# GpSimd scales weight pieces by multiplying two tensors, one of them a repeated column

## The chip, the cores and the metric

One core of one Trainium2 chip. The metric is the device time of one execution in microseconds, median of the runs. The kernel before took 574.97 us, median of 3 runs (567.21, 574.97 and 582.94). Engines are named as the profile names them: PE is TensorE's matmul side and PEld its weight loads, DVE is VectorE, ACT ScalarE, POOL GpSimd, SP the queue that issues most DMAs.

## The reference

One Flamingo-style layer: gated cross-attention, then a gated feed-forward layer with 8 experts of which each token uses 2. `x` is 8 x 256 x 256 (batch, tokens, width), the context 8 x 120 x 256.

```python
x = x + tanh(g_xattn[0]) * xattn(layernorm(x), ctx, w_q, w_kv, w_out, b_out)
x = x + tanh(g_ffn[0]) * ffn(layernorm(x), W1, W2, Wr)
# xattn: 16 heads of 64, softmax(q k^T / 8) v, then @ w_out + b_out
# ffn: the 2 best of 8 experts by softmax(x @ Wr^T), their weights renormalised,
#      y_e = silu(x @ W1[e]^T) @ W2[e]^T, out = sum of weight_e * y_e
# W1: (8, 1024, 256), W2: (8, 256, 1024)
```

Everything is float32 outside. The kernel keeps float32 accuracy with float16 matmuls: every operand is split into a high half and a low half (the rest that float16 could not hold), and a product is made of three matmuls.

## The kernel before

Attention runs over the 8 batches as one software pipeline: on each engine a list of steps is written out by hand inside a loop over p, and each step acts on batch p plus an offset. So order on an engine is fixed in the code, and engines meet through counting semaphores only. In the same loop the weights of the 8 experts are prepared, one expert per batch: SP loads `w1[q]` into `stage[0]` and `w2[q]` into `stage[1]` (each 128 x 2048 float32), ACT and PE find a bound from which DVE makes a power of two in `upw` (one column for W1, one for W2, the value repeated in all 128 partitions), ACT writes the high halves, and the low halves are made in chunks of 512 columns. In the trace this loop of weights covers roughly 46 to 285 us. After attention, 39 tiles of 128 gathered token rows go through the experts; tiles are added into `out` by an indirect DMA that accumulates, one after another.

Of an expert's eight chunks, four are made by DVE in one instruction each (line 1333: multiply by `upw`, subtract the high half) and four by POOL in two instructions each, in `split_low` of the GpSimd program (lines 630 to 641): line 637 scales the chunk in `stage` in place, then line 639 (W1) or 641 (W2) subtracts the high half and writes the float16 low half. A chunk is float32, 128 x 512. Between the two POOL waits on its own semaphore (`chain.link`), so that the second reads what the first wrote. With 8 experts there are 32 instructions on line 637, all in the loop.

POOL's other work in that loop, in program order around `split_low`: `p_low` (line 592, pT, the low half of the exponentials, a two-tensor subtraction of 120 x 512, eight per batch), `residual` (line 601), `scatter` (line 611, small indirect DMAs), and `norm2_factors` (lines 621 to 629, eight tiny instructions). What waits for them: PE's `values` (the matmuls o_bank<-v,pT) for `p_low`; SP's `store_w1` (line 436) for the low halves of W1, and `load_w` (lines 429 and 430), which fetches the next expert's W2 into `stage[1]`, for those of W2. ACT's `weight_sum` (line 885) then waits for that load.

```python
split_low(p + 7, 0, 1)
...
split_low(p + 7, 0, 3)
norm_factors(p + 8, 0)
p_low(p + 7, 0, 0)
...
p_low(p + 7, 0, 1)
...
split_low(p + 7, 1, 2)
...
split_low(p + 7, 1, 3)
p_low(p + 7, 1, 0)
```

Of the kernel before, what the change touches and what calls it, by code (L numbers as in the profile page):

```python
# [7 lines left out]
ALU = mybir.AluOpType  # L8
# [8 lines left out]
P = 128  # L17
# [150 lines left out]
def build(nc, x, ctxT, wq, wkv, wo, bo, gx, gf, w1, w2, wr, out, xn2_dram, table, w1_dram):  # L168
    ctx = ExitStack()
    with ctx:  # L170
# [3 lines left out]
        def sb(name, shape, dt, scope=ctx):  # L174
            return scope.enter_context(nc.sbuf_tensor(name, shape, dt))
# [26 lines left out]
        upw = [sb(f"upw{i}", [P, 2], F32) for i in range(2)]  # L202
# [179 lines left out]
        def w2_part(e, part, c, n=512):  # L382
            return w2s[:, e, part].rearrange("p c d -> p (c d)")[:, c:c + n]
# [138 lines left out]
        def _(pool):  # L522
            chain = Chain(pool, pool_chain)
# [107 lines left out]
            def split_low(q, i, k):  # L631
                if not 0 <= q < E:
                    return
                pool.wait_ge((w1_high, w2_high)[i][k // 2], q + 1)
                c = 512 * k
                chunk = stage[i][:, c:c + 512]
                chain.link(pool.tensor_scalar(chunk, chunk, upw[q % 2][:, i:i + 1], None, ALU.mult))  # L637
                if i == 0:
                    pool.tensor_tensor(w1_lo[:, k], chunk, w1_hi[:, c:c + 512], ALU.subtract).then_inc(w1_low[k], 1)
                else:  # L640
                    pool.tensor_tensor(w2_part(q, 1, c), chunk, w2_part(q, 0, c), ALU.subtract).then_inc(w2_low[k], 1)
# [58 lines left out]
            for p in range(-8, B + 3):  # L700
# [4 lines left out]
                tile_add(p + 4, 2)  # L705
                p_low(p + 6, 3, 1)
                split_low(p + 7, 0, 1)
                tile_gather(p + 6, 2)
                tile_gather(p, 12)
# [3 lines that stand above are left out]
# [8 lines left out]
                tile_add(p + 5, 0)  # L721
                constants(p + 8)
                split_low(p + 7, 1, 2)
                tile_add(p, 7)
                split_low(p + 7, 1, 3)
# [1364 lines left out]
```

## Time and profile before

| | |
|---|---|
| median of 3 runs | 574.97 us |
| lowest and highest run | 567.21 and 582.94 us |
| span of the profiled execution | 560.1 us |
| PE busy | 493.7 us (88%) |
| DVE busy | 370.2 us (66%) |
| ACT busy | 371.3 us (66%) |
| POOL busy | 363.9 us (65%) |

The span runs from the first to the last instruction; the page gives no total beside it, and the runs lie 7.1 to 22.8 us above it. Busy time is the union of an engine's instructions. A row of a timeline is: start in us, duration in us, engine, line, operation, output <- inputs with shapes, xcount, and in brackets the idle time before it and what ended it. A row of a group has, after the shapes, total busy us, mean ns of one, and the idle time before them. A row of the waits has total us, times, and the longest. The granted clock (PEclk) is a share of 2.4 GHz.

### The profile page before, as it was taken

How to read it: one execution, taken by the hardware profiler on the slowest of the kernel's cores; microseconds unless marked ns; L12 is line 12 of the kernel's file. 1: busy time of each engine (PE TensorE's matmuls, PEld its weight loads, DVE VectorE, ACT ScalarE, POOL GpSimd, SP SyncE). 2: the span in 40 equal slices, each digit the busy share in tenths (PEclk: the TensorE clock that was granted, in tenths of full speed). 3: DMA queues.
4: the chain of work that ended last, by engine and by line, in shares of the span. 5: the costliest groups of instructions: out<-in, count | busy, mean ns of one | idle time of the engine just before them, and what ended most of it. 6: DMA issues, size and time to landing. Idle time of an engine off the chain costs nothing. (4 is left out here: it accounts for less than half of the span.)

```text
span 560.1 us, 17891 instructions
## 1 busy us (share of the span) xinstructions
PE 493.7 (88%) x6630; PEld 438.3 (78%) x6631; DVE 370.2 (66%) x856; ACT 371.3 (66%) x576; POOL 363.9 (65%) x372
## 2 busy tenths in 40 slices
PE   2869799998999999798788997699999999999990
PEld 2757688887888879687567886689898898988980
DVE  5899999898889899699996664343444444343430
ACT  1838999998999899789546674245455464645530
POOL 5466979798989998788978642533544436344531
PEclk9979889999999999999689998799999999999996
DMA  7922506173553625263438598766787877778421
GB/s 286 392 77 84 175 12 219 48 244 59 175 127 119 178 97 168 33 212 73 130 148 201 153 287 145 208 185 186 214 259 201 259 207 232 229 224 244 112 30 17
DMA packets 34846, 93.13 MB, mean 166 GB/s; under 512 B 4967, under 2 KB 24565, under 8 KB 27490
## 3 DMA queue, kind: packets, MB, share of 16 engines
q1 hardware_dynamic: 25634, 81.86, 46.7%
q0 software_dynamic: 8576, 10.30, 9.5%
q8 instruction: 40, 0.66, 0.6%
q10 hardware_dynamic: 576, 0.14, 0.1%
q14 instruction: 20, 0.16, 0.1%
HBM read 74.17 MB, written 18.12 MB: 165 GB/s over the span
## 5 line engine op out<-in xcount | busy, mean ns | idle before, releaser
L689 POOL DMA_INDIRECT out<-yt,row_of x39 | 65.0, 1667 | 115.3 <-DMA out<-yt,row_of 96.5
L1642 PE MATMUL st_bank<-xsT,w_tile 128*128 128x128 f16 x1872 | 114.4, 221 | 4.3 <-issue 3.3
L1480 DVE SCALAR_TENSOR_TENSOR hT<-hf,h_scale,hT 128x512 f16<-128x512 f32 x78 | 58.6, 754 | 88.1 <-ACT hT L974 88.1
L1642 PEld LDWEIGHTS st_bank<-xsT,w_tile 128*128 128x128 f16 x1872 | 109.2, 99 | 7.0 <-issue 5.4
L1642 PE MATMUL o_bank<-w2s,hT 128*128 x936 | 109.9, 274 | 1.2 <-DVE yt L1489 1.1
L1642 PEld LDWEIGHTS o_bank<-w2s,hT 128*128 128x128 f16 x936 | 90.4, 99 | 12.4 <-issue 1.6
L968 ACT ACTIVATE hf<-st_bank,z_scale 128x512 f32<-128x512 f32 x78 | 52.9, 679 | 47.9 <-PE st_bank L1642 40.4
L592 POOL TENSOR_TENSOR pT<-pT 120x512 f16<-120x512 f32 x64 | 77.3, 1221 | 8.0 <-ACT pT L842 7.7
L974 ACT ACTIVATE hT<-hf,h_scale 128x512 f16<-128x512 f32 x78 | 56.3, 722 | 13.1 <-ACT hf L968 4.5
L637 POOL TENSOR_SCALAR stage<-stage,upw 128x512 f32<-128x512 f32 x32 | 55.9, 1748 | 10.5 <-ACT w_hi L941 10.4
L841 ACT ACTIVATE pT<-st_bank,exp_bias,logit_scale 120x512 f32<-120x512 f32 x64 | 50.0, 781 | 12.1 <-PE st_bank L1858 11.6
L842 ACT ACTIVATE pT<-st_bank,exp_bias,logit_scale 120x512 f16<-120x512 f32 x64 | 50.1, 783 | 0.0
L949 ACT ACTIVATE xsT<-max_pair 128x256 f16<-128x256 f32 x39 | 14.9, 382 | 48.8 <-PE max_pair L1896 44.7
L678 POOL DMA_INDIRECT xg<-xn,row_of x39 | 39.8, 1019 | 11.3 <-issue 8.9
L1778 PE MATMUL j_bank<-wos,oT 128*128 128x256 f16 x384 | 45.4, 272 | 0.3 <-DVE oT L1179 0.3
L1642 PE MATMUL o_bank<-v,pT 120*128 120x65 f16 x768 | 35.1, 197 | 11.7 <-DVE o L1367 9.6
L1642 PEld LDWEIGHTS o_bank<-v,pT 120*128 120x128 f16 x768 | 30.3, 99 | 18.2 <-issue 16.2
L611 POOL DMA_INDIRECT table<-entry,slot x32 | 32.9, 1027 | 14.2 <-DVE entry L1324 7.2
L1642 PE MATMUL j_bank<-xnT,wqs 128*128 128x256 f16 x336 | 41.0, 273 | 0.3 <-DVE oT L1179 0.3
L1778 PEld LDWEIGHTS j_bank<-wos,oT 128*128 128x128 f16 x384 | 36.4, 98 | 4.5 <-DVE oT L1179 0.4
L1344 DVE TENSOR_REDUCE max_pair<-max_pair 128x8 f32<-128x960 f32 x32 | 37.0, 1155 | 0.0
L1489 DVE TENSOR_SCALAR yt<-o_bank,gate_y 128x256 f32<-128x256 f32 x39 | 18.9, 483 | 25.4 <-PE o_bank L1642 25.2
(217 smaller groups left out, 966.5 us busy)
## 6 DMA issues: line engine op xcount, KB each, us to landing
w_tile<-w_split SPq DMA_DIRECT2D x39, 1024.0 KB, 5.2
stage<-in_w SPq DMA_DIRECT2D x16, 1024.0 KB, 5.1
w_split<-w_hi SPq DMA_DIRECT2D x8, 512.0 KB, 2.8
w_split<-stage SPq DMA_DIRECT2D x8, 512.0 KB, 3.9
out<-x SPq DMA_DIRECT2D x17, 128.0 KB, 5.4
xin<-in_x SPq DMA_DIRECT2D x8, 256.0 KB, 4.7
w2s<-in_wkv SPq DMA_DIRECT2D x2, 1024.0 KB, 12.2
xres<-in_x SPq DMA_DIRECT2D x16, 128.0 KB
```

The lines of the kernel that those rows point to most:

```text
L592: pool.tensor_tensor(pT[g % 2][:, 1, h, :], pT32[:, h, :], pT[g % 2][:, 0, h, :], ALU.subtract).then_inc(pT_low[h], 1)
L637: chain.link(pool.tensor_scalar(chunk, chunk, upw[q % 2][:, i:i + 1], None, ALU.mult))
L678: pool.indirect_dma_start(out=xg[t % XG][:], out_offset=None, in_=xn2_dram[0:rows], in_offset=bass.IndirectOffsetOnAxis(row_of[:, t:t + 1] ...
L689: pool.indirect_dma_start(out=out[0:rows], out_offset=bass.IndirectOffsetOnAxis(row_of[:, t:t + 1], 0), in_=yt[t % XG][:], in_offset=None, ...
L841: nc.scalar.activation(pT32[:, h, :], st_bank[h][0:M, :], ACT.Exp, bias=exp_bias[0:M], scale=logit_scale[0:M])
L842: nc.scalar.activation(pT[g % 2][:, 0, h, :], st_bank[h][0:M, :], ACT.Exp, bias=exp_bias[0:M], scale=logit_scale[0:M]).then_inc(exp_done[h ...
L968: nc.scalar.activation(hf[par][:, cols], z_bank[a][:], ACT.Silu, scale=z_scale[:, bass.ds(t, 1)]).then_inc(silu_done, 1)
L974: nc.scalar.activation(hT[par][:, 0, 4 * a:4 * a + 4, :], hf[par][:, cols].rearrange("p (c n) -> p c n", c=4), ACT.Copy, scale=h_scale[:, ...
L1344: ins = nc.vector.tensor_reduce(both[:, t].rearrange("p (h c) -> p h c", h=2), max_pair[:, :, 0:HP * M].rearrange("p h (c m) -> p h c m", ...
L1480: nc.vector.scalar_tensor_tensor(out=hT[par][:, 1, 4 * a:4 * a + 4, :], in0=hf[par][:, 512 * a:512 * a + 512].rearrange("p (c n) -> p c n" ...
L1642: ins = pe.matmul(out, lhs[i](a), rhs[i](c), start=(i == 0 and a + c == 0), stop=(i == n - 1 and a == 1))
L1778: ins = pe.matmul(dst[:, 0:D], oT[t][:, a, ic, :], wos[:, c, ic, :], start=(ic + a + c == 0), stop=(ic == IC - 1 and a == 1))
```

## The change

Line 637, the scaling of a chunk on POOL, is written as a multiplication of two tensors. Its second operand is the same column of `upw`, presented as 128 x 512 by repeating the one element of each partition (a step of zero). Output, place, wait and order are the same; so are the results, bit for bit, since the factor is a power of two. No instruction is added, removed or moved on any engine: 32 instructions change their kind.

```diff
                 c = 512 * k
                 chunk = stage[i][:, c:c + 512]
-                chain.link(pool.tensor_scalar(chunk, chunk, upw[q % 2][:, i:i + 1], None, ALU.mult))
+                chain.link(pool.tensor_tensor(chunk, chunk, upw[q % 2][:, i:i + 1].to_broadcast([P, 512]), ALU.mult))
                 if i == 0:
                     pool.tensor_tensor(w1_lo[:, k], chunk, w1_hi[:, c:c + 512], ALU.subtract).then_inc(w1_low[k], 1)
```

## Rows read from the trace of the kernel before

**Rows 1.** The page: the span, and busy us (share) x instructions by engine.

```profile
span 560.1 us, 17891 instructions
PE 493.7 (88%) x6630; PEld 438.3 (78%) x6631; DVE 370.2 (66%) x856; ACT 371.3 (66%) x576; POOL 363.9 (65%) x372
```

**Rows 2.** Busy time by stretch: stretch, its length, then each engine.

```profile
core 0: us, PE busy (x) PEld busy (x) DVE busy (x) ACT busy (x) POOL busy (x), PEclk, DMA share, GB/s
46.00:285.00 239.00, 222.83 (x3238) 190.07 (x3236) 213.50 (x521) 209.89 (x326) 212.46 (x215) 0.96 0.44 132
...
160.00:190.00 30.00, 29.48 (x450) 25.67 (x448) 27.21 (x70) 27.84 (x45) 28.15 (x30) 1.00 0.52 141
```

**Rows 3.** Groups of instructions on POOL, shapes kept apart.

```profile
L637 POOL TENSOR_SCALAR stage<-stage,upw 128x512 f32<-128x512 f32 x32 | 55.9, 1748 | 10.5 <-ACT w_hi L941 10.4
L641 POOL TENSOR_TENSOR w2s<-stage,w2s 128x512 f16<-128x512 f32 x16 | 19.0, 1187 | 1.3
L601 POOL TENSOR_TENSOR xres<-xres,bout 128x256 f32<-128x256 f32 x16 | 11.3, 725 | 1.0 <-DVE bout L1160 0.9
L580 POOL TENSOR_SCALAR_AFFINE_SELECT sel<-sel 128x480 bf16<-128x480 bf16 x4 | 2.4, 608 | 0.4
```

**Rows 4.** Line 637: ns least/median/most, first and last start.

```profile
L637 POOL TENSOR_SCALAR stage<-stage,upw x32: 1553/1568/2137, 46.2 to 277.3; 128x512 f32<-128x512 f32 x32
```

**Rows 5.** What PE waited for, 46 to 285 us: total, times, longest.

```profile
PE o_bank L1642 <- DVE o L1367: 6.0, 3, 3.2
...
PE o_bank L1642 <- POOL pT L592: 0.5, 1, 0.5
```

**Rows 6.** What POOL waited for, 46 to 285 us.

```profile
POOL stage L637 <- ACT w_hi L941: 10.4, 2, 8.7
POOL pT L592 <- ACT pT L842: 7.7, 9, 3.5
...
POOL ln_b L621 <- DVE mv L1256: 2.6, 1, 2.6
POOL table L611 <- DVE entry L1324: 2.1, 4, 0.6
```

**Rows 7.** Timelines of two batches: exponentials, their low halves, PE's use.

```profile
155.87 1.16 POOL L592 TENSOR_TENSOR pT<-pT 120x512 f16<-120x512 f32 x1 [0.55 <-ACT pT L842]
...
166.16 2.72 POOL L592 TENSOR_TENSOR pT<-pT 120x512 f16<-120x512 f32 x2
...
168.99 0.53 PE L1642 MATMUL o_bank<-v,pT 120*128 120x65 f16 x12 [0.52 <-issue]
...
185.73 0.77 ACT L842 ACTIVATE pT<-st_bank,exp_bias,logit_scale 120x512 f16<-120x512 f32 x1
...
186.95 1.16 POOL L592 TENSOR_TENSOR pT<-pT 120x512 f16<-120x512 f32 x1
```

**Rows 8.** Timelines of SP's queue and ACT: the next W2 load.

```profile
183.48 0.33 SPq L430 DMA_DIRECT2D stage<-in_w  x1
...
191.87 1.91 ACT L885 ACTIVATE w2s<-stage 128x2048 f16<-128x2048 f32 x1 [1.66 <-DMA stage<-in_w]
```

**Rows 9.** DVE's chunks beside POOL's: two timelines, then groups of line 1333.

```profile
116.62 1.56 POOL L637 TENSOR_SCALAR stage<-stage,upw 128x512 f32<-128x512 f32 x1
...
117.16 0.74 DVE L1333 SCALAR_TENSOR_TENSOR w2s<-stage,upw,w2s 128x512 f16<-128x512 f32 x1
...
86.60 1.16 POOL L641 TENSOR_TENSOR w2s<-stage,w2s 128x512 f16<-128x512 f32 x1
86.82 1.49 DVE L1333 SCALAR_TENSOR_TENSOR w2s<-stage,upw,w2s 128x512 f16<-128x512 f32 x1
...
87.74 2.00 POOL L637 TENSOR_SCALAR stage<-stage,upw 128x512 f32<-128x512 f32 x1
...
L1333 DVE SCALAR_TENSOR_TENSOR stage<-stage,upw,w_hi 128x512 f16<-128x512 f32 x16 | 15.9, 991 | 0.3 <-ACT w_hi L941 0.3
L1333 DVE SCALAR_TENSOR_TENSOR w2s<-stage,upw,w2s 128x512 f16<-128x512 f32 x16 | 15.3, 958 | 0.0
```

## The prediction

> **What bounds the kernel now.** I read the page first, then busy time by stretch, then the waits, then timelines around the changed line. The page says that PE is busy 493.7 us of a span of 560.1 [rows 1], far more than any other engine. All 32 instructions of line 637 start between 46.2 and 277.3 us [rows 4], so the stretch that counts is 46 to 285 us. In it PE is busy 222.8 of 239 us, DVE 213.5, ACT 209.9 and POOL 212.5: four engines nearly full, PE fullest. In its calmest part, 160 to 190 us, PE is busy 29.48 of 30 us and POOL 28.15 [rows 2]. So a batch takes about 30 us because PE has about 29.5 us of work in it, and POOL keeps pace with little room.
>
> Nearly full is not the same as in the way. PE's waits in the stretch name DVE first: 6.0 us for the normalised outputs o. POOL is named once, with 0.5 us [rows 5]. One more belongs to it though the row says "issue": the pair of pT instructions that starts at 166.16 ends at 168.88, and PE's matmul on pT starts at 168.99 after 0.52 us of idleness [rows 7]. POOL itself waits: 1.7 us for ACT's high halves (10.4 less the 8.7 before the first chunk), 7.7 us for ACT's exponentials, 2.6 and 2.1 us for DVE [rows 6], 14.1 us in all. That is POOL's slack in the stretch.
>
> **What the change removes and adds.** Removed: 32 multiplications by a scalar per partition, median 1.568 us [rows 4]; their mean is 1.748 and their sum 55.9 us [rows 3]. The 0.18 us between mean and median is time lost to DVE: the instruction at 87.74 took 2.00 us while a DVE instruction of two SBUF inputs was still running, the one at 116.62 took 1.56 [rows 9].
>
> Added: 32 two-tensor multiplications with a repeated column. The trace has no such instruction. Its nearest rows are two-tensor instructions of POOL: 1.187 us mean for 128x512 with a float16 output (line 641), and 0.725 us for 128x256 all in float32 (line 601) [rows 3]. From these two the cost per element is at most (1.187-0.725)/256, 1.8 ns, so an all-float32 instruction of 512 comes to 0.725+0.46, 1.19 us. I take 1.2 us: the nearest row has the same shape, the same place in the queue, and reads the same chunk. Bound from below: one pass over 480 elements took 0.608 us (line 580) [rows 3], so 0.65 for 512, if the repeated column costs nothing. Bound from above: if the repeated column is as dear as what the old instruction did on top of a second stream, 1.57+1.19, 2.76 us. I stay with 1.2, because a step of zero still is a regular stream, and the row above differs from it in nothing else.
>
> The Trainium skill speaks against the change: GPSIMD Engine Reference, section 4.1, calls one-input work on GpSimd roughly line rate, and section 3.1 puts two-input work at about 2.6 cycles per element at 1.2 GHz. Worked out from that page, as an estimate, the old instruction would take 0.43 us and the new one 1.11, and POOL would gain 22 us of work where by the rows it loses 12. The trace agrees on the two-input kind (1.187 us) and disagrees on the other by a factor of over three (1.568 us).
>
> POOL's busy time thus falls by 32 x (1.57-1.20), 11.8 us. How much reaches the end?
>
> - *Low halves of the exponentials.* Four scalings stand in each batch, so POOL runs 1.5 us earlier behind them, until it meets an input that isn't there. It soon does. At 155.87 it waited 0.55 us for ACT already before the change, so nothing is left of the 1.5 us behind that point, nor at the matmul at 168.99. At 186.95 it started 0.45 us after ACT was done (185.73+0.77 is 186.50), so 0.45 us survive there [rows 7]. The gain turns into a longer wait for ACT. PE's two waits for POOL, 1.04 us, are the most there is; I take 0.5 us.
> - *The next W2 load.* SP issues it at 183.48, when POOL's last W2 chunk is done, and ACT waits 1.66 us for it before 191.87 [rows 8]. The load would start up to 1.5 us earlier and ACT would be that much ahead, but ACT isn't what PE names. I take 0.5 us over the whole stretch.
> - *DVE.* Line 1333 needs two SBUF inputs, and takes 0.74 us when free. Started inside the scaling at 116.62 it still took 0.74; started inside the two-tensor instruction at 86.60 it took 1.49, ending 0.55 after that one [rows 9]. Two-tensor instructions on POOL hold DVE off nearly to their end, the scaling in this place doesn't. The new instruction is of the kind that does. About ten of the 32 DVE chunks start inside a scaling now; of these some six would still fall in its first us, and lose some 0.3 us each: 2 us on DVE, which has 25.5 us idle in the stretch. Of what reaches PE I take 0.5 us lost. That today's chunks average 0.991 and 0.958 us instead of 0.74 (31.2-23.7, 7.5 us) shows the size of this effect as it is.
>
> The sum is -0.5-0.5+0.5, about -0.5 us; I round to -1, since the lead on POOL can also take a wait out of a batch that I didn't follow. Against the profiled execution this is 559.1 of a span of 560.1. The runs lie 7.1 to 22.8 us above that span, with a median 14.9 above; nothing in the change touches what lies outside the span, so I carry the difference to the median: 574.97-1, 574.0 us.
>
> **The rivals.**
>
> *A, the lead on POOL frees more (faster).* In the stretch PE idles 239-222.8, 16.2 us, and its clock is at 0.96 of 2.4 GHz [rows 2], which means that for part of it 1.2 GHz was granted: another 0.04 x 239, some 9.6 us of lost work. If half of both came back because POOL's earlier finish loosens DVE and ACT, the time would be 575-13, 562 us. For it: all four engines are so full that delays of one are passed to the next. Against it: POOL is behind hardly any of PE's waits [rows 5]. It decides if PE's idle time in the stretch falls below some 8 us.
>
> *B, the new instruction costs more than the old (slower).* If the repeated column makes the two-tensor form slow, POOL gets longer. Its slack is 14.1 us [rows 6], 0.44 us an instruction; so from 2.0 us each POOL becomes the bound. At the upper bound, 2.76 us, POOL gains 38.1 us, less 14.1 of slack: 24 us slower, 599 us. For it: no row has a step of zero. Against it: the rows of two streams are all near 1.2 us for 512 elements. By the page's figures above POOL's extra 22 us, less 14.1, would give about 583 us; the trace has refuted that price for the old instruction.
>
> *C, DVE is held off more (a little slower).* If all ten chunks that now pass freely inside a scaling are each held for 0.75 us as the one at 86.82 was (1.49-0.74), DVE loses 7.5 us. DVE is what PE waits for most [rows 5]; with half passed on it is +4, 579 us. It decides if the mean of line 1333 rises above 1.2 us. The Trainium skill, SBUF — State Buffer, section "Who interferes with whom", says that a VectorE instruction with two SBUF inputs contends with any GpSimd instruction that reads SBUF, as an exclusive lock for the whole instruction. By that rule the old scaling would have held DVE off as well and nothing would change; the row at 117.16 disagrees.
>
> *D, no effect at all,* since PE is the bound: 575 us. It can't be told from the forecast, and I count it there.
>
> **How the numbers follow.** The forecast with D has 0.75, A 0.07, B 0.06, C 0.12. The runs of this kernel spread from 567 to 583 us, so a median of a few moves by some 5 us by itself, and about 2% (11.5 us) is what such a measurement can tell from no change. The range has to hold that spread around 574 and case C, not the far end of B nor all of A: 564 to 583 us. Faster by over 2% is most of A and a little of the spread, 0.09; slower is B and a sliver of C, 0.09; the rest, 0.82, is the same.
>
> **What would show it.** In the profile of the changed kernel: line 637 as a two-tensor instruction with a median near 1.2 us (1.15 to 1.3; above 2.0 is B); POOL busy in the stretch some 12 us lower and POOL's waits for ACT's pT longer than 7.7 us by most of that; PE busy about the same 223 us and idle near 16; line 1333 at a mean of 1.0 to 1.1 us (above 1.2 is C). The prediction would be wrong if PE's waits for DVE shrank or grew by several us, or if the granted clock in the stretch moved from 0.96, since each hundredth is worth 2.4 us.

## The result and the profile after

The changed kernel took 572.29 us, median of 6 runs (569.79 to 575.68); the kernel before, run beside it, 575.74 us (567.21 to 582.94, 6 runs with the 3 shown earlier). The ratio of the two is 1.0098, 95% interval 1.0052 to 1.0145: about 1% slower. Ratios, here and below, are made only from the fast executions, those near the fastest of their kernel, which is why this one is above 1 though the plain medians stand the other way round; the profiles of W1 only, twice and five chunks below are of slow ones. By the bound of 2% this is the same time; against its own interval it moved, and not the way I had forecast. Executions of one kernel spread by 1 to 3% here, so the runs that follow carry the verdict, not this ratio alone.

First, what POOL gained. Two rows of groups of the changed kernel (name, shapes, count | total us, mean ns | idle before), which answer to [rows 3], and one with least, median and most ns, which answers to [rows 4]:

```profile
L637 POOL TENSOR_TENSOR stage<-stage,upw 128x512 f32<-128x512 f32 x32 | 36.0, 1125 | 5.6 <-ACT w_hi L941 5.6
L639 POOL TENSOR_TENSOR stage<-stage,w_hi 128x512 f16<-128x512 f32 x16 | 21.2, 1327 | 1.3
...
L637 POOL TENSOR_TENSOR stage<-stage,upw x32: 1032/1040/1528, 43.3 to 275.6; 128x512 f32<-128x512 f32 x32
```

The new instruction takes 1.04 us, cheaper than I had assumed. POOL's 32 scalings fell from 55.9 to 36.0 us. The page's row of busy time, and the stretch of 46 to 285 us (columns as in [rows 2]):

```profile
PE 496.4 (88%) x6630; PEld 440.4 (78%) x6631; DVE 372.3 (66%) x856; ACT 371.2 (65%) x576; POOL 345.4 (61%) x372
...
46.00:285.00 239.00, 218.56 (x3206) 185.82 (x3205) 216.11 (x517) 206.84 (x322) 193.30 (x213) 0.96 0.44 132
```

POOL is 19 us less busy in the stretch (212.46 before), but PE did less in the same time: 218.56 us busy where it was 222.83, so its idle time rose from 16.2 to 20.4 us. (In two copies of the kernel before, described below, PE was busy 221.6 us in the same window, so about 1 of the 4.3 us is chance.) DVE, with the same instructions, is busier: 216.11 after 213.50. Now the waits, first POOL's, then PE's (total us, times, longest), beside [rows 6] and [rows 5]:

```profile
POOL pT L592 <- ACT pT L842: 25.7, 25, 3.5
```

```profile
PE j_bank L1747 <- DVE nmp L1355: 6.0, 2, 5.9
PE o_bank L1642 <- DVE o L1367: 5.7, 3, 3.1
...
PE o_bank L1642 <- POOL pT L592: 0.6, 1, 0.6
```

POOL's wait for ACT's exponentials grew from 7.7 to 25.7 us. That is 18.0 of the 19.9 us it had saved: POOL reached its inputs earlier and stood there. PE's wait for POOL is what it was, 0.6 us. Its wait for DVE grew, by the one for nmp, which was 2.2 us before.

Why DVE grew is in the chunks it makes itself, line 1333. The rows of the kernel after that answer to the groups in [rows 9], then one of its chunks and what POOL did meanwhile:

```profile
L1333 DVE SCALAR_TENSOR_TENSOR stage<-stage,upw,w_hi 128x512 f16<-128x512 f32 x16 | 18.9, 1181 | 0.3 <-ACT w_hi L941 0.2
L1333 DVE SCALAR_TENSOR_TENSOR w2s<-stage,upw,w2s 128x512 f16<-128x512 f32 x16 | 16.1, 1007 | 0.0
...
104.84 1.04 POOL L637 TENSOR_TENSOR stage<-stage,upw 128x512 f32<-128x512 f32 x1
105.00 1.42 DVE L1333 SCALAR_TENSOR_TENSOR stage<-stage,upw,w_hi 128x512 f16<-128x512 f32 x1
105.96 1.49 POOL L639 TENSOR_TENSOR stage<-stage,w_hi 128x512 f16<-128x512 f32 x1
```

The 32 chunks took 35.0 us in all, 31.2 before; free of POOL they would take 23.7 (32 x 0.74). The chunk at 105.00 starts inside the two-tensor scaling and takes 1.42 us, almost twice its free time, and then POOL's next instruction pays as well: 1.49 us instead of 1.16, for DVE is now in its way. In the kernel before, all ten chunks that started inside a scaling took 0.74 us, as the one at 117.16 in [rows 9]; in the changed kernel eight start inside one, with a mean of 1.19 us.

That comparison mixes two things, since the ten all started 0.53 us or later into a scaling, and six of the eight at 0.54 us or earlier. In copy 1 of the kernel before (described below) two chunks did start early in the old scaling:

```profile
77.65 1.56 POOL L637 TENSOR_SCALAR stage<-stage,upw 128x512 f32<-128x512 f32 x1
77.70 1.18 DVE L1333 SCALAR_TENSOR_TENSOR stage<-stage,upw,w_hi 128x512 f16<-128x512 f32 x1
...
230.70 1.57 POOL L637 TENSOR_SCALAR stage<-stage,upw 128x512 f32<-128x512 f32 x1
231.04 0.89 DVE L1333 SCALAR_TENSOR_TENSOR stage<-stage,upw,w_hi 128x512 f16<-128x512 f32 x1
```

Both end 0.74 us, a free duration, behind the moment at which the scaling had run 0.49 us (77.70+1.18-0.74-77.65, and the same for the other pair). So the old form holds DVE too, but only for the first 0.49 of its 1.57 us. For the chunk at 105.00 the same sum gives 105.00+1.42-0.74-104.84, 0.84 us, and 0.84 or 0.85 for each of the seven of the eight that were lengthened: the new form holds DVE for 0.85 of its 1.04 us. The new form is 0.53 us shorter and its hold 0.36 us longer.

The 7.0 us between the two spans (560.1 and 567.1) can't be read as the price of the change. PE reaches the same matmul, the first on nmp of the last batches, at 277.72 us before and at 277.67 after, and the whole difference of the spans lies behind it, where not one instruction of line 637 runs. That the two profiles stand level at this matmul is chance as well: the kernel before began the stretch with line 637 late, at 42.65 us where the changed kernel began at 39.19 (the rows are below), and made up for it. The copies show what both are worth.

### The profile page after: what moved, and what is told of

The parts are those of the page before. It is cut to its first block, busy times and chain, and to the rows that moved or that the text cites. A ratio compares the mean times of both kernels' runs of the same rounds, so it can differ in the third digit from the quotient of the medians.

```text
span 567.1 us, 17891 instructions
## 1 busy us (share of the span) xinstructions
PE 496.4 (88%) x6630; PEld 440.4 (78%) x6631; DVE 372.3 (66%) x856; ACT 371.2 (65%) x576; POOL 345.4 (61%) x372
## 4 chain that ended last, share of the span: by engine, by line
DMA 33%; PE 30%; issue 13%; DVE 10%; POOL 7%; ACT 6%; another core or an unknown queue 1%; POOLq 0%; SPq 0%; ACTq 0%; DVEq 0%
DMA out<-yt,row_of 30%; PE j_bank L1642 9%; PE o_bank L1642 4%; PE st_bank L1855 3%; PE j_bank L1778 3%; PE max_pair L1834 2%; DMA xg<-xn,row_of 2%; PE j_bank L1738 2%; ACT w2s L885 2%; PE st_bank L1642 2%; POOL table L611 1%; PE j_bank L1648 1%; DMA w2s<-in_wq 1%; POOL xg L678 1%; ACT pT L842 1%
## 5 line engine op out<-in xcount | busy, mean ns | idle before, releaser
L1642 PE MATMUL st_bank<-xsT,w_tile 128*128 128x128 f16 x1872 | 117.0, 223 | 1.6 <-issue 1.4
L1642 PEld LDWEIGHTS st_bank<-xsT,w_tile 128*128 128x128 f16 x1872 | 111.7, 100 | 4.5 <-issue 3.0
L592 POOL TENSOR_TENSOR pT<-pT 120x512 f16<-120x512 f32 x64 | 78.4, 1233 | 26.0 <-ACT pT L842 25.7
L678 POOL DMA_INDIRECT xg<-xn,row_of x39 | 39.7, 1018 | 11.3 <-issue 9.5
L1642 PEld LDWEIGHTS o_bank<-v,pT 120*128 120x128 f16 x768 | 30.9, 100 | 20.0 <-issue 18.3
L637 POOL TENSOR_TENSOR stage<-stage,upw 128x512 f32<-128x512 f32 x32 | 36.0, 1125 | 5.6 <-ACT w_hi L941 5.6
L1642 PEld LDWEIGHTS j_bank<-xnT,wqs 128*128 128x128 f16 x336 | 31.8, 98 | 4.7 <-issue 0.8
```

The lines of the kernel that those rows point to most:

```text
L592: pool.tensor_tensor(pT[g % 2][:, 1, h, :], pT32[:, h, :], pT[g % 2][:, 0, h, :], ALU.subtract).then_inc(pT_low[h], 1)
L678: pool.indirect_dma_start(out=xg[t % XG][:], out_offset=None, in_=xn2_dram[0:rows], in_offset=bass.IndirectOffsetOnAxis(row_of[:, t:t + 1] ...
L1642: ins = pe.matmul(out, lhs[i](a), rhs[i](c), start=(i == 0 and a + c == 0), stop=(i == n - 1 and a == 1))
```

## The experiments

I had two theories. Theory 1: the two-tensor scaling holds DVE off, and that costs more than POOL's shorter time brings. Its rivals: nothing happened and the difference is chance (theory 2 below); or POOL's being early is what does harm, by shifting transfers and low halves.

The measure that tells them apart best isn't the total time but the time PE takes between two fixed matmuls, one at the start of the stretch in which line 637 runs (`max_pair<-kT,qT`, start of the row) and one at its end (`j_bank<-identb,nmp`, the row that waits for DVE). I call it PE's stretch. Rows of four kernels, two of each: the kernel before, the changed one, its first copy, and the padded kernel of below.

```profile
42.65 0.80 PE L1834 MATMUL max_pair<-kT,qT 64*128 64x120 f16 x24
...
277.72 0.27 PE L1747 MATMUL j_bank<-identb,nmp 128*128 128x128 bf16 x2 [2.22 <-DVE nmp L1355]
```

```profile
39.19 0.80 PE L1834 MATMUL max_pair<-kT,qT 64*128 64x120 f16 x24 [0.41 <-DVE nmp L1355]
...
277.67 0.37 PE L1747 MATMUL j_bank<-identb,nmp 128*128 128x128 bf16 x2 [5.87 <-DVE nmp L1355]
```

```profile
40.45 0.80 PE L1834 MATMUL max_pair<-kT,qT 64*128 64x120 f16 x24 [0.41 <-DVE nmp L1355]
...
282.83 0.37 PE L1747 MATMUL j_bank<-identb,nmp 128*128 128x128 bf16 x2 [5.86 <-DVE nmp L1355]
```

```profile
39.90 0.80 PE L1836 MATMUL max_pair<-kT,qT 64*128 64x120 f16 x24 [0.41 <-DVE nmp L1357]
...
280.30 0.37 PE L1749 MATMUL j_bank<-identb,nmp 128*128 128x128 bf16 x2 [5.97 <-DVE nmp L1357]
```

They give 235.1, 238.5, 242.4 and 240.4 us. In the table "held" is what the 32 chunks of line 1333 took above 0.74 us each, whatever POOL did meanwhile; then come what POOL waited for pT between 46 and 285 us, PE's longest wait for nmp, and, within the stretch, PE's idle time and the part of it that DVE ended. (The kernel named five chunks has 24 such instructions.)

| kernel | PE's stretch, us | held, us | POOL waits for pT, us | PE waits for nmp, us | PE idle, us | of it for DVE, us |
|---|---|---|---|---|---|---|
| before | 235.1 | 7.5 | 7.7 | 2.2 | 15.3 | 9.6 |
| before, copy 1 | 235.2 | 5.9 | 8.1 | 4.8 | 17.1 | 9.9 |
| before, copy 2 | 234.7 | 6.1 | 7.3 | 4.8 | 17.1 | 10.1 |
| after | 238.5 | 11.3 | 25.7 | 5.9 | 20.3 | 14.3 |
| after, copy 1 | 242.4 | 9.5 | 25.7 | 5.9 | 21.9 | 16.0 |
| after, copy 2 | 238.5 | 10.8 | 25.7 | 5.9 | 20.5 | 13.1 |
| padded | 240.4 | 10.4 | 4.5 | 6.0 | 21.7 | 13.3 |
| W1 only | 238.6 | 8.0 | 17.9 | 3.3 | 19.1 | 11.7 |
| W2 only | 236.9 | 8.5 | 17.8 | 3.4 | 15.7 | 9.6 |
| full stream | 237.4 | 11.1 | 16.3 | 3.7 | 16.1 | 11.0 |
| twice | 249.1 | 16.2 | 2.1 | 5.4 | 28.2 | 17.6 |
| no scaling | 236.5 | 3.7 | 64.1 | 3.4 | 16.9 | 11.5 |
| five chunks | 237.1 | 7.6 | 10.1 | 5.9 | 18.3 | 9.9 |

In all three profiles of after PE idles 3.2 us or more longer than in any of before, and nearly all of that ends with DVE. But the stretch doesn't follow the held time kernel by kernel: full stream is held as much as after, with a stretch 1.1 us shorter and PE idle 4.2 us less, and no scaling, held least, has a longer stretch than the kernel before.

**Copies: what is chance.** The kernels before and after, unchanged.

> The kernel before, unchanged, run as if it were a change: it tells how far two sets of runs of one kernel stand apart. Both theories expect a ratio of 1.00 to the kernel before; any distance from 1.00 is the floor under which no other ratio of these runs says anything. Spans that differ by 3 to 7 us from 560.1 between executions would mean that much of the 7.0 us between the two profiled spans is chance.

> The changed kernel, unchanged, in more rounds. Theory 1 (the two-tensor scaling holds DVE off, and that costs more than POOL's shorter time brings): ratio 1.005 to 1.015, mean of line 1333 above 1.0 us, POOL's waits for ACT's pT near 25 us again. Theory 2 (nothing happened: the 7 us lie in single idle stretches of one execution, such as the 2.7 us before 305.92 on DVE that no engine ended): ratio 0.995 to 1.005, and the idle stretches of 300 to 350 us fall elsewhere this time.

Measured beside one set of runs of the kernel before (561.66 us, 557.53 to 575.85, 11 runs): the copy of before 566.99 us (566.33 to 573.15, 6 runs), ratio 1.0142 (1.0078 to 1.0206); the copy of after 572.07 us (571.09 to 573.20, 6 runs), ratio 1.0211 (1.0163 to 1.0259). One kernel against itself stood 1.4% apart. So no single ratio of 1% says anything here, the first one included; copy against copy, after is 572.07/566.99, 0.9% slower. The spans of the three profiles of the kernel before are 560.1, 563.7 and 566.6 us: one kernel spreads by 6.5 us, nearly the 7.0 us between the first two spans of the case. Behind the nmp matmul the spans left 282.4, 288.0 and 291.4 us before and 289.4, 286.6 and 287.5 after: no difference. One such piece of chance is an idle stretch of DVE for which the profile names no instruction that ended it. In the changed kernel, and in copy 1 of the kernel before:

```profile
305.92 0.18 DVE L1364 RECIPROCAL rsum<-o_bank 128x4 f32<-128x4 f32 x1 [2.68 <-remote]
```

```profile
303.98 0.18 DVE L1364 RECIPROCAL rsum<-o_bank 128x4 f32<-128x4 f32 x1 [2.44 <-remote]
```

In the first profile of the kernel before the same instruction had waited 0.12 us. PE's stretch is steadier: within 0.5 us over three profiles of before, and 3.3 to 7.6 us longer in all three of after (which spread by 3.9 us among themselves). By this measure the theory of no effect falls; the total times alone wouldn't refute it.

> The changed kernel once more, beside the kernel before once more on the same chip. Theory 1: stretch of PE 238 us or more, DVE held off in its chunks by 9 us or more in all, ratio to the copy of the kernel before 1.005 to 1.015.

> The kernel before once more. Theory 1: stretch of PE near 235 us, DVE held off in its chunks by 6 to 8 us in all. A ratio to the other runs of the same kernel as far from 1 as the 1.014 of the last copy would mean that a set of runs of one kernel can stand apart by more than the whole effect.

On another chip, beside 35 runs of the kernel before (568.59 us, 563.40 to 577.64): copy 2 of before 568.17 us (12 runs), ratio 0.9994 (0.995 to 1.0037); copy 2 of after 571.86 us (562.57 to 579.27, 12 runs), ratio 0.9997 (0.9938 to 1.0057), which rests on 5 of its 12 executions. The expected ratio of 1.005 to 1.015 was missed by that measure; by the medians of all runs after is 3.3 to 3.7 us, 0.6%, above before. PE's stretch, 238.5 against 234.7 us, says the same as that.

**One half of the chunks at a time.** The edit of W1 only; W2 only has `i == 1` in place of `i == 0`.

```diff
-                chain.link(pool.tensor_scalar(chunk, chunk, upw[q % 2][:, i:i + 1], None, ALU.mult))
+                chain.link(pool.tensor_tensor(chunk, chunk, upw[q % 2][:, i:i + 1].to_broadcast([P, 512]), ALU.mult)
+                           if i == 0 else
+                           pool.tensor_scalar(chunk, chunk, upw[q % 2][:, i:i + 1], None, ALU.mult))
```

> Only the 16 chunks of W1 are scaled by two tensors, the 16 of W2 by a scalar per partition as before. In the changed kernel it is the W1 group of line 1333 that rose (median 0.968 to 1.220 us), the W2 group hardly (0.752 to 0.802). Theory 1: nearly all of the loss is here, ratio as that of the whole change, 1.005 to 1.015. Theory 2: 1.00. POOL busy falls by 16 x 0.53, 8 us.

> Only the 16 chunks of W2 are scaled by two tensors. Theory 1: POOL is 8 us shorter and DVE hardly held off more, so ratio 0.995 to 1.002. Theory 2: 1.00 as well; what tells them apart is the distance to the kernel that changes W1 alone, 0.5 to 1.5% by theory 1, under 0.3% by theory 2.

W1 only took 568.82 us (557.43 to 576.56, 6 runs, without a ratio), W2 only 572.64 us (570.17 to 574.53, 6 runs), ratio 1.0214 (1.0157 to 1.0271). I had expected the loss in the W1 half, since there line 1333 grew most, and W2 only near 1.00. By the times it came out the other way, by 0.7% at a floor of 1.4%; by PE's stretch W1 only is the longer one, 238.6 against 236.9 us, with PE idle 19.1 against 15.7 us. The two measures contradict each other, so these two kernels don't tell which half carries the loss. Held are 8.0 and 8.5 us, where the kernel before has 5.9 to 7.5.

**POOL as late as before, only the kind changed.** The kernel padded. A first form of it, with two writes of a larger scratch tile as the filler, had no room in SBUF and gave no time.

```diff
                 chain.link(pool.tensor_tensor(chunk, chunk, upw[q % 2][:, i:i + 1].to_broadcast([P, 512]), ALU.mult))
+                chain.link(pool.tensor_tensor(idle_space[:], onesb[:, 0:1], minus_half[:, 0:1], ALU.pow))
```

> The changed kernel, and behind each scaling POOL does a power of one element into a scratch column, which reads next to nothing. The power rows of before (0.73 us for 2 columns, 1.05 for 4) put it near 0.57 us, so scaling and power together last about as long as the old scaling (1.57 us), and POOL's schedule is that of before; only the kind of the scaling differs. Theory 1 (the two-tensor scaling holds DVE off): DVE chunks of line 1333 still average above 1.0 us, PE takes 237 us or more for the stretch between the two matmuls that lay 235.1 and 235.2 us apart in the two profiles of the kernel before and 238.5 and 242.4 in those of the changed one, and the time is within 0.5% of the changed kernel's. Rival (the loss comes from POOL being early): back to 235 us and to the time of before.

This is the run that tests whether the loss needs POOL to be early.

```profile
L639 POOL TENSOR_TENSOR idle_space<-onesb,minus_half x32: 547/556/1084, 45.1 to 280.0; 128x1 f32<-128x1 bf16 x32
...
46.00:285.00 239.00, 216.81 (x3188) 184.44 (x3187) 213.09 (x511) 206.35 (x318) 213.47 (x244) 0.97 0.43 130
```

The filler took 0.556 us and POOL is as busy as before the change, 213.47 us against 212.46; its wait for pT is even shorter, 4.5 us. Yet the chunks of DVE are held off by 10.4 us, PE's stretch is 240.4 us, and the time 572.90 us (568.53 to 577.76, 12 runs), ratio 1.0089 (1.0052 to 1.0126), as that of after. The loss came without any lead of POOL, so the rival falls. It isn't a pure test of the kind, though. The filler reads two tensors itself, and of the 10.4 us held only 1.3 belong to chunks that started inside the new scaling (3.6 of 11.3 in after, none of 7.5 before). Chunks that started inside the subtractions (lines 641 and 643 here, 639 and 641 before), which are the same instructions in both kernels, were held 6.4 us here and 3.8 to 4.9 in the three profiles of before. So a good part of the loss comes from where POOL's and DVE's instructions meet, and no run here holds that fixed while the kind changes.

**More of the same hold, and none.**

```diff
                 chain.link(pool.tensor_tensor(chunk, chunk, upw[q % 2][:, i:i + 1].to_broadcast([P, 512]), ALU.mult))
+                ones_4 = onesb[:].unsqueeze(1).to_broadcast([P, 4, P])
+                parts = chunk.rearrange("p (r c) -> p r c", c=P)
+                chain.link(pool.tensor_tensor(parts, parts, ones_4, ALU.mult))
```

> The changed kernel, and behind each scaling POOL multiplies the chunk by one, a second two-tensor instruction over the same chunk, results unchanged. POOL's pair before a subtraction takes about 2.2 us instead of 1.57 before the change: 20 us more POOL than in the kernel before, where POOL's waits left 14.1. Theory 1: DVE is held off by still more, and POOL becomes late: 3 to 8% slower than the kernel before is too much, 1.5 to 4% (8 to 22 us) is expected. If POOL and its hold on DVE didn't matter: within 1%.

> Line 637 is left out altogether (the chunk isn't scaled before the subtraction), POOL is 56 us shorter than before the change and nothing in its place holds DVE off. Theory 1: DVE chunks average 0.95 us or less, PE idles less than the 15 us of before, time 0 to 1.5% below the kernel before. If POOL's lead by itself did harm, this one, with the largest lead, would be slower than the changed kernel.

Twice took 585.12 us (574.04 to 587.54, 4 runs) beside 566.80 us (559.82 to 573.84, 7 runs) of before: 18 us or 3.2% slower by the medians (without a ratio), with 16.2 us held and a stretch of 249.1. In its profile POOL's slack is gone too (2.1 us of waiting for pT is left), and PE's wait for POOL's pT, 0.6 us in after, is 2.7 us. So this one shows both prices together, that of rival B and the hold. No scaling took 565.84 us (562.61 to 575.82, 4 runs), ratio 1.0014 (0.9921 to 1.0108): DVE is held least (3.7 us), POOL is 56 us shorter, and the time is that of the kernel before. PE's stretch, 236.5 us, isn't below 235 either. POOL's old length was not in the way, and taking the hold away below what it was before brings nothing. What keeps the stretch near 235 us isn't shown: PE still idles 16.9 us in it, 11.5 of them until DVE is done.

**Why 1.04 us.** The kernel full stream.

```diff
-                chain.link(pool.tensor_tensor(chunk, chunk, upw[q % 2][:, i:i + 1].to_broadcast([P, 512]), ALU.mult))
+                factor = minus_half[:].unsqueeze(1).to_broadcast([P, 32, TT])
+                parts = chunk.rearrange("p (r c) -> p r c", c=TT)
+                chain.link(pool.tensor_tensor(parts, parts, factor, ALU.mult))
```

> The second operand of the scaling is 16 columns of the constant -0.5, repeated 32 times, so it isn't one repeated element any more (the scaling by upw is left out in this kernel, a chunk is multiplied by -0.5). If the repeated single column is what makes the new instruction 1.04 us, cheaper than the 1.16 us of line 641, this one takes 1.15 to 1.25 us. If instead it is cheap because all its operands are float32, it takes 1.04 again. Time within 1% of the changed kernel either way.

```profile
L639 POOL TENSOR_TENSOR stage<-stage,minus_half x32: 1263/1278/1809, 43.8 to 275.0; 128x512 f32<-128x512 f32 x32
```

A second operand with different float32 elements side by side costs 1.278 us (median), the repeated element 1.040, and a float16 or bfloat16 one lies between: 1.16 us is the median of line 641's instructions and of the multiplication by one in the kernel above. So it isn't the float32 operands that make the new instruction cheap; the single repeated element is what is left. One difference stays untested: this operand comes in rows of 16 elements, the repeated element in one row of 512. Rows of 128 cost nothing extra in twice (1.164 us, against 1.158 for line 641). Its time, 570.03 us (567.06 to 578.16, 4 runs), ratio 1.009 (0.9997 to 1.0183), and stretch, 237.4 us, are near those of after.

**Using what POOL gained.** The kernel five chunks. POOL takes chunk 1 of W2 over from DVE.

```diff
 # DVE's list
-                split_low(p + 1, 1, 1)
 # POOL's list
+                split_low(p + 7, 1, 1)
                 split_low(p + 7, 1, 2)
```

> The changed kernel, and POOL takes a fifth of the eight chunks of an expert from DVE (chunk 1 of W2), which uses the time that POOL has gained: POOL +8 x 2.2 = 18 us, DVE -8 x 1.0 = 8 us, and one two-SBUF-input instruction of DVE less per batch that can be held off. If DVE is what PE waits for, PE's stretch falls to 233 to 236 us and the time to that of the kernel before or 1% below it. If DVE doesn't matter, as the changed kernel, or slower since POOL is as full as before the change.

It took 574.22 us (566.86 to 578.90, 12 runs), ratio 1.0075 (1.0029 to 1.0122). DVE lost 8 instructions, and PE's stretch is 237.1 us, 1.4 less than in the two nearer profiles of after, but not at the 233 to 236 I had expected. The time isn't better. No kernel of this study is faster than the kernel before beyond the spread.

## Why the prediction was wrong

- *PE is the bound, POOL is near but not in the way.* Right for POOL: 56 us less of it gave nothing, and PE's wait for pT stayed at 0.6 us. Of PE I said too much: 9.6 of its 15.3 idle us in the stretch end with DVE, so what DVE loses can reach the end.
- *The new instruction takes 1.2 us.* Too high: 1.04. The term was 11.8 us of POOL's time, from medians; in the same way it measured 16.9, and by the sums of all 32 it was 19.9. It had no weight for the end. Rival B, a new instruction dearer than the old, didn't happen; its mechanism was seen only when POOL did the work twice.
- *The lead on POOL turns into a wait for ACT.* Right, and nearly whole: 18.0 us more waiting. The 0.5 us that I let survive for pT didn't show.
- *The W2 load starts earlier, 0.5 us.* Of no account. ACT no longer waits for that load in the stretch, but neither does it in the two copies of the kernel before, so the 1.66 us were chance.
- *DVE loses 2 us and 0.5 reach PE.* This is the step that failed, in its size. The mechanism was the one of rival C. The chunks lost 3.8 us between the two first profiles (35.0-31.2), and 3.4 to 5.4 between the after ones and the copies of before; the mean of line 1333 came out at 1.094 us, inside my 1.0 to 1.1. I had six chunks lose 0.3 us each. Seven lost 0.51 on average, because I left them where they start in the old scaling, 0.53 us or later, while in the changed kernel four of them start within its first 0.2 us and lose 0.7. Above all I took a quarter of the loss to reach PE: PE's waits for DVE grew by 3.0 us or more (13.1 to 16.0 after 9.6 to 10.1) and its stretch by 3.3. DVE's other instructions on SBUF change as well, and they stand in short dependent chains. Where the experts of the early tiles are found, the row of xn2T starts at 268.24 before and at 267.16 after, and the reciprocal behind the chain at 274.43 and 274.38: 6.2 us and 7.2 us for the same work. Rows of after from it:

```profile
267.16 0.68 DVE L1264 COPY xn2T<-j_bank 128x512 f32<-128x512 f32 x1
...
268.39 1.00 DVE L1404 TENSOR_SCALAR small<-iota,small 128x8 f32<-128x8 f32 x1
269.43 1.08 DVE L1405 TENSOR_TENSOR small<-small 128x8 f32<-128x8 f32 x1
...
272.71 1.76 DVE L1424 CAST expert_of<-expert_f 128x13 int32<-128x13 f32 x1
274.38 0.17 DVE L1364 RECIPROCAL rsum<-o_bank 128x4 f32<-128x4 f32 x1
```

  Lines 1404, 1405 and 1424 work on a handful of elements each. In the profile of before they took 0.48, 0.17 and 0.63 us, and two others of the same chain (lines 1408 and 1420) 1.08 and 1.11, which are down to 0.16 and 0.26 here. So the chain pays for where it falls beside POOL's instructions, 1.0 us net. PE stands behind it for nmp: 5.9 us in all three profiles of after, 2.2 to 4.8 in those of before. PE's stretch grew by 3.3 us or more, where I had 0.5, and so came true what I had named as a sign of being wrong, a growth of PE's waits for DVE by several us. How much of that came through the 32 chunks and how much through such chains, the runs don't separate.
- *Rivals.* C had 0.12 and was the right one, with +4 us; measured in PE's stretch +3.3 to +7.6, in time +3.7 us by one pair of copies and +5.1 by the other. That its +4 fits is partly luck: its sign, a mean of line 1333 above 1.2 us, didn't show, and it had ten chunks held for 0.75 us each. The weights were wrong: the trace said in [rows 9] that two-tensor instructions hold DVE where the old scaling didn't, and in [rows 5] that PE waits for DVE and not for POOL. Together these two speak for "slower", and I let a gain on an engine that nobody waited for outweigh them.
- *The rule on the shared port.* The Trainium skill, SBUF — State Buffer, section "Who interferes with whom", says that a VectorE instruction with two SBUF inputs contends with a GpSimd instruction that reads SBUF. The traces agree for two-tensor instructions on POOL, and for the scalar-per-partition scaling in its first 0.49 us; behind that they disagree: none of the ten chunks was held. The prediction's "for the whole instruction" is said there of VectorE's two-port modes; here even the two-tensor form let DVE go 0.19 us before its end.
- *What lies outside the span.* I took the 7.1 to 22.8 us between the first span and the runs to lie outside the span. The runs recorded since lie 1.8 to 3.6 us above their own spans, so most of that distance is a span that changes from one execution to the next. The forecast carries only a difference, so its 1 us isn't touched by this.
- *The range*, 564 to 583 us, held 572.29, and the plain medians even moved the forecast way, 575.74 to 572.29; both are luck, for the range is as wide as the spread of the runs, and the forecast of 1 us less had its sign against it.

## What to carry over

When an instruction on GpSimd gets shorter by changing its kind, ask what the new kind does to VectorE while it runs: look in the trace for a VectorE instruction that started inside one of either kind, and compare it with its free duration. A saving on an engine that nobody waits for is returned as that engine's own waiting; a hold on the engine that TensorE waits for can reach the end. And when ratios of 1% are at stake, run the kernel against itself first, and compare the time between two fixed instructions of the trace around the change, which here was steady to 0.5 us in three profiles of the kernel before while its totals spread by 3%; in the changed kernel a slower granted clock moved it by some 2 us, so read PE's busy and idle time in it too.

## What was unexpected of the hardware

- On GpSimd a multiplication by a scalar per partition (1.57 us for 128x512 float32) is slower than the three two-tensor forms measured at the same size: 1.04 us with one repeated element, 1.16 with a 16-bit second operand, 1.28 with a float32 one.
- A VectorE instruction with two SBUF inputs, 0.74 us when free, was held by both forms, but not for as long: until the scalar form had run 0.49 of its 1.57 us (two cases in copy 1 of before), and until the two-tensor form had run 0.85 of its 1.04 us (seven cases in after). Started later inside either, it took 0.73 to 0.75 us in all profiles of the two kernels.
- Tiny VectorE instructions pay as much as large ones: 8 to 13 elements a partition, 1.00 to 1.76 us. Why the CAST at 272.71, which has one input, took 1.1 us more than in the kernel before is left open; no run was made for it.
- After's copy 1 has a stretch of 242.4 us against 238.5 in the other two. Its granted clock was 0.50 (1.2 GHz) from 232.4 to 239.2 us, where that of after was 1.00; PE had just idled 3.6 us for DVE's o, against 2.4 in after, and the 12 matmuls behind took 2.75 us instead of 1.48. That makes PE's busy time in the stretch 220.5 us instead of 218.2, and its waits for o 8.1 instead of 5.7 us make up most of the rest.
